# A decoder layer on one core: the first sequence's drives made by GpSimd from broadcast rows, and its scores in four row groups

## Time and profile before

| | us |
|---|---|
| median of 3 runs | 455.75 (455.47 to 456.05) |
| the profiled execution | 456.57 |
| its span | 454.8 |
| TensorE (PE) busy | 385.3 |
| VectorE (DVE) busy | 301.9 |
| ScalarE (ACT) busy | 195.5 |
| GpSimd (POOL) busy | 192.1 |

### The profile page before, as it was taken

One profiled execution on the slowest core, in us unless ns is written; L12 is line 12 of the kernel. 1 busy time (PEld: TensorE's weight loads), 2 busy tenths in 40 slices (PEclk: granted clock), 3 DMA queues, 4 the chain that ended last, 5 costly groups with the idle time before them and its releaser, 6 DMA issues.

```text
span 454.8 us, 7173 instructions
## 1 busy us (share of the span) xinstructions
PE 385.3 (85%) x2552; PEld 331.1 (73%) x2552; DVE 301.9 (66%) x639; ACT 195.5 (43%) x470; POOL 192.1 (42%) x207
## 2 busy tenths in 40 slices
PE   3867878977959678899898888988979999999993
PEld 2545666756747567789777778976859899899982
DVE  6445467557587478988937899882799984552233
ACT  2691545636250555354335555334545522321110
POOL 6012635436522176753314677221657831151131
PEclk9958798989976968999999999999998999999998
DMA  7542251000012111321030132002013300000000
GB/s 212 210 183 77 81 182 74 25 1 23 2 36 46 51 46 47 94 94 35 1 97 25 46 117 100 19 1 95 24 48 119 113 1 0 2 25 0 2 0 23
DMA packets 12339, 27.03 MB, mean 59 GB/s; under 512 B 1800, under 2 KB 3088, under 8 KB 12048
## 3 DMA queue, kind: packets, MB, share of 16 engines
q1 hardware_dynamic: 11296, 24.74, 16.4%
q10 hardware_dynamic: 1008, 1.84, 1.2%
HBM read 25.39 MB, written 1.18 MB: 58 GB/s over the span
## 4 chain that ended last, share of the span: by engine, by line
PE 51%; DVE 24%; issue 12%; ACT 6%; POOL 4%; DMA 1%; SPq 1%; DVEq 0%; POOLq 0%; ACTq 0%
PE xf L1059 15%; PE gen L1059 13%; PE a2p L1059 11%; PE ret L1059 5%; PE acc L1059 5%; DVE gen L1612 4%; DVE ret L1612 3%; DVE sc L1629 2%; DVE ring L1620 2%; DVE ring L1679 2%; PE xf L1138 1%; DVE fth L1875 1%; DMA wattn_sb<-in_wattn 1%; POOL ring L561 1%; ACT L776 1%
## 5 line engine op out<-in xcount | busy, mean ns | idle before, releaser
L1059 PE MATMUL xf<-am,wsplit 128*128 128x256 f32 x672 | 95.3, 293 | 2.0 <-DVE work L1886 1.5
L1059 PEld LDWEIGHTS xf<-am,wsplit 128*128 128x128 f32 x672 | 87.2, 195 | 4.4 <-DVE work L1886 3.4
L561 POOL TENSOR_TENSOR ring<-decay,brow 128x512 f32<-128x512 f32 x48 | 61.6, 1302 | 17.0 <-PE acc L1059 16.5
L670 POOL TENSOR_TENSOR work<-work,ratioT 128x256 f32<-128x256 f32 x28 | 20.9, 746 | 98.6 <-DVE work L1886 91.2
L1059 PE MATMUL a2p<-work,wff_sb 128*128 128x256 f32 x224 | 58.1, 382 | 0.5 <-POOL work L670 0.5
L1875 DVE SCALAR_TENSOR_TENSOR fth<-fth,xf 128x256 f32<-128x256 f32 x56 | 23.2, 415 | 46.1 <-ACT fth L1003 45.8
L1059 PE MATMUL xf<-x2s,wsplit 128*128 128x256 f32 x336 | 52.6, 309 | 0.2
L1003 ACT ACTIVATE fth<-xf 128x256 f32<-128x256 f32 x56 | 21.0, 375 | 73.4 <-PE xf L1059 71.9
L1059 PEld LDWEIGHTS xf<-x2s,wsplit 128*128 128x128 f32 x336 | 46.7, 204 | 1.8 <-DVE work L1886 0.7
L1059 PE MATMUL acc<-ident,ring 128*128 128x128 f32 x256 | 38.9, 284 | 9.0 <-DVE ring L1620 8.8
L1059 PEld LDWEIGHTS a2p<-work,wff_sb 128*128 128x128 f32 x224 | 39.6, 192 | 4.5 <-POOL work L670 0.9
(11 more groups left out here) (278 smaller groups left out, 751.6 us busy)
## 6 DMA issues: line engine op xcount, KB each, us to landing
brow<-bc_dram SPq DMA_DIRECT2D x24, 256.0 KB, 3.6
crow<-bc_dram SPq DMA_DIRECT2D x24, 256.0 KB, 3.3
work<-in_wsp SPq DMA_DIRECT2D x3, 896.0 KB, 9.0
wff_sb<-in_wff SPq DMA_DIRECT2D x2, 896.0 KB, 7.6
am<-bc_dram SPq DMA_DIRECT2D x1, 1536.0 KB, 7.6
wattn_sb<-in_wattn SPq DMA_DIRECT2D x1, 1280.0 KB, 5.7
xT_sb<-in_xT SPq DMA_DIRECT2D x4, 256.0 KB, 2.7
out_y<-keep ACTq DMA_DIRECT2D x4, 256.0 KB, 2.5
```

What stands on the lines that cost most here:

```text
L561: pool.tensor_tensor(ring[:, i % RING], du_of(b)[:, j].unsqueeze(1).broadcast_to([P, UN, S]), brow[:, c % 2], ALU.mult).then_inc(sem["driv ...
L670: pool.tensor_tensor(xs[:, n % 4], fq[:, m % 2], ratioT[:], ALU.mult).then_inc(sem["xs_ready"], 1)
L1059: return pe.matmul(o, l, r, skip_group_check=True, **kw)
```

## The change

All of it is in `first`. The work for B's columns goes (`rates`, `flip_inputs`, `drive`, `drive_columns`). SyncE loads rows 0 to 3 of B broadcast into `brow`, one load ahead of each load of C; later pairs of rows are loaded from ScalarE's queue (`drive_rows`). GpSimd makes all 16 drives into `ring` (`drive_unit`), each two units ahead of its product with C, and VectorE's scan works in place, from SBUF. Of the products with C, VectorE takes six (`FIRST_DVE`), right behind the scan. The scores of a half (four heads pairs) are taken together, in four row groups of the array into four banks, in even slots only, behind the values; five banks rotate.

```diff
+FIRST_DVE = (2, 5, 8, 11, 14, 15)
-PRELUDE = [... ("DBL", 0, 0), ("DT", 0, 0), ("BT", 0, 1), ("V", 0, 2), ("KN", 0, 1),
-           ("SC", 0, 1), ("SC", 1, 0), ("SC", 2, 2), ("SC", 3, 1), ("Q", 1, 0)]
+PRELUDE = [... ("DBL", 0, 3), ("DT", 0, 4), ("V", 0, 0), ("KN", 0, 1),
+           ("SC", 0, 2), ("SC", 1, 3), ("SC", 2, 4), ("SC", 3, 0), ("Q", 1, 1)]
...
-    return (2, 1, 0)[[u for u in ROTATED[:k + 1] if u not in OWN_BANK].index(use) % 3]
+    return (2, 3, 4, 0, 1)[[u for u in ROTATED[:k + 1] if u not in OWN_BANK].index(use) % 5]
...
             for k, (s0, s1) in enumerate(((0, 2 * UN), (2 * UN, DS))):
+                sp.dma_start(brow[:, k], of(bc_dram, 0)[k * UN:(k + 1) * UN].partition_broadcast(P)
+                             ).then_inc(sem[f"b_in{k}"], 16)
                 sp.dma_start(first_c[:, s0:s1], ...
...
 GpSimd, first:
+                drive_unit(b, 0)
+                drive_unit(b, 1)
                 decayed_queries(0)
...
                     for unit in FIRST_UNITS.get(i, ()):
-                        first_times_c(b, unit)
+                        if unit + 2 < UNITS:
+                            drive_unit(b, unit + 2)
+                        if unit not in FIRST_DVE:
+                            first_times_c(b, unit)
...
 ScalarE:
-            def drive_columns(b, c):
...
+            def drive_rows(b, c):
+                need(act, "drive_ready", b, 2 * c - 2)
+                act.dma_start(brow[:, c % 2], of(bc_dram, b)[c * UN:(c + 1) * UN].partition_broadcast(P)
+                              ).then_inc(sem[f"b_in{c % 2}"], 16)
...
 TensorE:
-            def scores(s, r):
-                t = r // 2
-                banks = [gen_use("SC", PAIRS * s + 2 * r + k) for k in range(2)]
+            def scores(s, t):
+                banks = [gen_use("SC", PAIRS * s + 4 * t + w) for w in range(4)]
                 for chunk in range(2):
-                    for k in range(2):
-                        w = 2 * (r % 2) + k
+                    for w in range(4):
                         rows_ = slice(32 * w, 32 * w + 32)
...
-                rates(b)
                 token_values(0)
                 token_keys(0)
-                flip_inputs(b)
-                drive(b, 0)
-                drive(b, 1)
                 scores(0, 0)
-                scores(0, 1)
                 project(1, "Q", wq)
...
-                    if s < B:
-                        scores(s, r)
                     if r == 2 and s < B:
                         values(s, 0)
                     if r == 0 and s <= B:
                         values(s - 1, 1)
+                    if s < B and r % 2 == 0:
+                        scores(s, r // 2)
                     for unit in FIRST_UNITS.get(i, ()):
-                        if unit + 2 < UNITS:
-                            drive(b, unit + 2)
                         if unit > 0:
                             add_states(b, unit - 1)
...
 VectorE, first_scan:
-                dve.tensor_tensor_scan(flat(ring[:, i % RING]), flat(decay[:, i % 2]), flat(drives[i % 2][:]), 0.0,
+                unit = ring[:, i % RING]
+                dve.tensor_tensor_scan(flat(unit), flat(decay[:, i % 2]), flat(unit), 0.0,
                                        ALU.mult, ALU.add).then_inc(sem["state_ready"], 1)
+                if i in FIRST_DVE:
+                    c = i // 2
+                    first_c_read(dve, i)
+                    need(dve, "state_ready", b, i + 1)
+                    dve.tensor_tensor(unit, unit, first_c[:, c * UN:(c + 1) * UN], ALU.mult).then_inc(sem["first_out"], 1)
```

More of the change, by code:

```diff
@@ L88, in gen_order @@
         s, r = turn(i)
-        if s < B:
-            uses += [("SC", PAIRS * s + 2 * r), ("SC", PAIRS * s + 2 * r + 1)]
+        if s < B and r % 2 == 0:
+            uses += [("SC", PAIRS * s + 2 * r + w) for w in range(4)]
         if r == 0:
@@ L407, in need_out, with first_turn, first_c_read @@
         def need_out(eng, b, units):
[L409 to L412, removed]
+            need(eng, "out_dve", b - 1, units)
+        def first_turn(i):
+            return [k for k in range(UNITS) if (k in FIRST_DVE) == (i in FIRST_DVE)].index(i)
+        def first_c_read(eng, i):
+            mine = [k for k in range(UNITS) if (k in FIRST_DVE) == (i in FIRST_DVE)]
+            if i == mine[0]:
+                eng.wait_ge(sem["c_first0"], 16)
+            if i == [k for k in mine if k >= 4][0]:
+                eng.wait_ge(sem["c_first1"], 16)
         def of(ap, b):
@@ L902, in first @@
                         if unit % 2 == 0 and unit // 2 + 2 < UNITS // 2:
-                            drive_columns(b, unit // 2 + 2)
+                            drive_rows(b, unit // 2 + 2)
                     if r == 3 and 0 < s <= B:
@@ L1084, in xf_free @@
                 else:
-                    need(pe, "state_ready", 0, UNITS)
+                    need(pe, *emptied(previous(3, FILLED["OUT", B - 1])))
             def project(s, name, w):
@@ L1110, in low_rank @@
                 last.then_inc(sem["gen_filled"], 1)
-            def rates(b):
-                g = gen_use("BT", b)
-                need(pe, "u_ready", b, 1)
-                for t in range(NT):
-                    for j in range(2):
-                        last = mm(g[:, t * DS:(t + 1) * DS], u[:, j, t * P:(t + 1) * P], w_xp[:, j, DR:DR + DS],
-                                  start=(j == 0), stop=(j == 1))
-                last.then_inc(sem["gen_filled"], 1)
-            def flip_inputs(b):
-                need(pe, "du_ready", b, 1)
-                for t in range(NT):
-                    for j in range(2):
-                        last = pe.transpose(acc[:, t, j * P:(j + 1) * P], du_of(b)[:, j, t * P:(t + 1) * P], ident[:])
-                last.then_inc(sem["duT_filled"], 1)
-            def drive(b, i):
-                j, c = i % 2, i // 2
-                need(pe, "state_ready", b, max(i - 1, 0))
-                for s in range(UN):
-                    if j == 0:
-                        pe.wait_ge(sem["dub_ready"], NT * (c * UN + s + 1))
-                    for t in range(NT):
-                        last = pe.transpose(drives[i % 2][:, s, t * P:(t + 1) * P],
-                                            dub[(c * UN + s) % 4][:, t, j * P:(j + 1) * P], ident[:])
-                last.then_inc(sem["drive_ready"], 1)
             def step_size(b):
@@ L1186, in start_y @@
                 need(pe, "y_init", b, 2)
-                if fb is None:
-                    pe.wait_ge(sem["duT_ready"], 1)
-                else:
+                if fb is not None:
                     need(pe, "am_ready", fb, 3)
```

55 lines of the change are left out of this document (15 added, 40 removed).

## The result

The changed kernel takes 458.06 us (median of 4, 457.35 to 458.79) where the one before takes 455.75 (455.47 to 456.05): ratio 1.0051 [1.0029, 1.0072] (in brackets the 95% interval). Measured again, with 12 executions of it and 35 of the one before, the ratio was 1.0026 [1.0006, 1.0047]. It is slower by 0.3 to 0.5%, where I had forecast 1.4% faster. The profiled execution took 457.35 us, its span 455.6, against 456.57 and 454.8. A ratio is to executions of the kernel before taken beside it and leaves out those over 1.5% above a kernel's fastest, so where a kernel spreads wider than that, the ratio of the medians over all of its executions is given too.

A forecast was written before the change was run, and what follows sets the result against it. A loop of TensorE and VectorE, TensorE the larger part, was taken to bound `first`. Gains of 16.3 us less debits of 10.5 gave 5.8, checkpoints 6.6; 6.3 taken off 455.75 gave 449.4, range 442.5 to 458.

The forecast's parts named there:

- First checkpoint: First mask product of slot 0, at 40.78 us before the change: forecast at 34.9 to 36.9, gain taken 4.8 us.
- Second and third: First mask products of slots 2 and 6, at 57.49 and 85.65 us before: a gain of 3 us taken at each.
- Fourth: Slot 10, at 115.73 us before: gain 9.8 with full-clock V and no further waits, 3 if neither; taken 5.5.
- Fifth: Slots 11 to 13: no second score visit before V, +1.1 us; slot 13 nothing; gain 6.6 at the end of `first`.
- The clock term: TensorE idles more, so one projection more runs at 1.2 GHz: a loss of 1.5 us, bounds -1.5 and 6.
- Turns: 25 VectorE instructions wait for a busy GpSimd in `first`: a loss of 4 us on the chain, bounds 0 and 10.
- the scans don't take turns: Rival: VectorE's scans from SBUF run unhindered by GpSimd; gain 12.0 us, time 443.8, chance 0.18.
- Order on GpSimd: In odd slots the drive of u+2 precedes the product with C of u: a loss of 3 us, bounds 0 and 6.4.
- VectorE's products: Six products with C on VectorE, less the GpSimd product TensorE no longer awaits: a loss of 2 us, bounds 0 and 3.6.
- The gross of the scores: Score visits saved by four side-by-side groups, 6.5 us, plus the covered wait for the next keys, 3 us.
- the shared path fills up: Rival: GpSimd and VectorE turns fill slots 2 to 9, in-order queues leave idle time; slower, 458.6 us, chance 0.20.
- Eaten by the clock or a bank: Rival: score visits' waits for four banks and the clock each take 2.5 us more; gain 1.3, 454.4 us, chance 0.11.

The follow-up runs named there:

- e9: Changed kernel plus 32 unread TensorE products ahead of waiting additions: median 453.76 us over six executions, ratio to before 0.9942 (0.9891 from four).
- e1: Changed kernel with `Z` of sequence 0 and V of sequence 3 moved to PSUM banks 0 and 1: 456.39 us, ratio to before 0.9972.
- e5: Changed kernel with the scores as before (two at a time, three banks, ahead of the values): 462.42 us, ratio to before 1.0113.
- e6: Changed kernel with the old scores and sequence 0's decays in PSUM, so scans have one SBUF input: 459.17 us, ratio to before 1.0041.
- e3: Changed kernel with GpSimd's product with C of u ahead of the drive of u+2: 454.66 us, ratio to before 0.9939.
- e4: Changed kernel with all 16 products with C on GpSimd, none on VectorE: 457.63 us, ratio to before 1.0024.
- e8: Changed kernel with two banks moved, feed-forward loads earlier and GpSimd's product before its drive: median 454.79 us, ratio 0.9964 over eleven executions, 0.9861 from three.
- fourth mend: TensorE's state additions moved behind the projections: alone on the changed kernel 458.06 us, ratio 1.0034; with bank, weights and order edits 448.90 us, 0.9822.
- e14: Kernel before the change plus 16 unread TensorE products where it waits for VectorE: 457.82 us, ratio to before 0.9994.
- e2: Changed kernel with the feed-forward weight loads issued earlier, at about 30 us: 457.55 us, ratio to the changed kernel's predecessor 1.0000.

## Why the prediction was wrong

In short: the sum gave the scores' part 9.5 us and it brought 2.8 to 4, and the drives' part was to lose 3.7 us and lost 5.2. The scores' gain was there, and two terms took it back: a bank in slots 10 and 11, which the sum had at nothing, and the clock, which it had at 1.5 us. By its own steps:

- **First checkpoint** (slot 0 at 34.9 to 36.9): 33.69. The gain in the prelude was there and larger.
- **Second and third** (54.5, about 82.65): 54.56 and 83.02. Right, but slot 2 was right by luck, through two errors: the addition of unit 1 came at 45.91, not 48.4, and the low clock took 2.6 us of it back (e9: 51.28).
- **Fourth** (slot 10 at 110.2): 112.51. I said "gain 5.5" between 3 "if neither" and 9.8; it was 3.2, next to the bound without full clock. The sign of being wrong that I had named, a gain that shrinks through slots 2 to 9, didn't show (2.9 to 3.2): the loss lay in front of that stretch and behind it.
- **Fifth**, the step that failed worst: "Slots 11 to 13 have no second score visit. In slot 11 one stood before V: +1.1." From slot 10's mask product on it was -2.8, 3.9 us off. I took the second visit's time away and didn't ask what use each bank now follows. I had walked the five-bank rotation only for the score visits' own waits (the rival), not for the uses behind them. e1 shows it: 0.5 to 0.8%. With the bank mended the same stretch is 1.3 us shorter than before (14.3 for 15.6), so the +1.1 itself was about right.
- **The clock term**, "one projection more at 1.2 GHz than before: 1.5", bounds -1.5 and 6. With filler the changed kernel gains 4 to 6 us, the kernel before none. The value was in the upper part of the bounds: the change makes TensorE wait 23.6 us for the products with C, where it waited 10.7 for scans, and the chunk state and K projection of slot 1, `Z`'s turns and V of slot 11 each ran at the low level behind a wait, not one projection.
- **Turns**, 4 us: e5 to e6 gives 3.3, in the kernel with the old scores. Scans do take turns; "the scans don't take turns" (443.8) is refuted.
- **Order on GpSimd**, 3 us: e3 gives 3.4 to 4. It was a loss that the prediction named, and an edit of two lines mends it.
- **VectorE's products**, 2 us: no difference by e4, between bounds of 0 and 3.6.
- **B's rows** "hidden": not in slot 4, 2.75 us late by 2.6 MB of other loads that I hadn't put beside it, worth at most 0.3 to 0.5%.
- **The gross of the scores**, 6.5 + 3: four groups do run side by side. A visit of 16 products in four banks takes 1.1 us, as two groups did. Rows of the visit in slot 10:
```profile
111.27 0.48 PE L1054 MATMUL gen<-qm,x 32*128 32x256 f32 x1
...
111.28 0.48 PE L1054 MATMUL xf<-qm,x 32*128 32x256 f32 x2
...
112.03 0.38 PE L1054 MATMUL xf<-qm,x 32*128 32x256 f32 x2
```
  But the scores' part brought 2.8 to 4 us (e5 against the changed kernel), and 6.4 with its bank order mended (e5 to e1, 1.0113 to 0.9972). The drives' part I had nearly right: 6.8 less the debits of 10.5 is 3.7 slower, and e5 is 5.2 slower.

Of the rivals, "the shared path fills up" gave 458.6, next to the result, by a mechanism that didn't occur where it was put: slots 2 to 5 took 28.5 us, not 32.4, and slots 6 to 9 29.5, not 32.2. Only in the window of slot 1 was GpSimd busy nearly throughout (13.4 of 16 us). The rival's 27.4 us of turns for slots 6 to 9 also counts six drives where the order of units has five there; with five it is 26.1, and the rival's time about 457. "Eaten by the clock or a bank" named the right causes, at 2.5 us each; the bank took about that (2.5 to 3.6), in another slot than I had it, and the clock 4 to 6. The mends don't add up as the parts do: bank 0.5 to 0.8%, order 0.9% and weights at most 0.5% make 1.4 to 2.2% by sum, and e8 gives 0.6 (over all executions) to 1.65% (by its three fastest). What stays open is why e8 has two groups of executions, and why the fourth mend helps only beside the other three.

## What to carry to other kernels

When a change re-deals rotating buffers, write down for every use behind it which use it now follows and who empties that one, and when; the uses that nobody edited are the ones that get hurt. When work moves off the busiest engine, list the places where that engine will now wait longer, and price at the low clock what stands behind each of them, not behind one; filler ahead of the waits tells whether the price is real. Of two queued instructions, put first the one whose result another engine stands for.

## What the runs showed of the hardware

- Four row groups of 32x128 by 256 columns, each into its own bank, take the time of two: 16 products in 1.1 us, eight in 1.13.
- A scan with both inputs in SBUF beside GpSimd work took 1.47 to 1.50 us on the mean and 2.15 at most; with one input in PSUM 1.21.
- Matmuls that nothing reads made a kernel faster: 32 more of them, 4 to 6 us less (e9). In the kernel before, 16 of them made none (e14).
- A load of 256 KB took 8.24 us to land beside 2.6 MB of other loads; in e2, without them, the six of its kind took 3.1 us at the median and 5.5 at most.
- Kernels of which only `first` differs spent 285.0 to 289.3 us in the identical passes after it, most of them 286.0. The 289.2 of e1 goes with two more stretches of low clock. Executions of the kernel before lay between 455.1 and 460.8.
